# A Mamba decoder block on one core: two of five scan steps get dt*u*B by transposes, the other products are one operation of 1024, and the task planner gets new durations

## What is computed

```python
x = layernorm(x + mamba(mamba(x)))            # two Mamba layers, D_INNER 512, 64 states
x = layernorm(x + attention(x, ctx))          # 256 keys, one head, Wq Wk Wv Wo
x = layernorm(x + experts(x))                 # 8 experts, hidden 1024, the two best weighted

# inside a Mamba layer, for each of 512 channels d and 64 states s:
dt = softplus(...)                            # per channel and time
h[t] = exp(dt[t] * A[d, s]) * h[t-1] + dt[t] * u[t] * B[t, s]
y[t] += h[t] * C[t, s]
```

## Time and profile before

| | |
|---|---|
| median of 3 runs | 3817.08 us (3805.78 to 3820.71) |
| profiled execution | 3814.09 us |
| its span, first to last instruction | 3812.3 us |
| mean granted TensorE clock | 0.894 |
| VectorE, TensorE, ScalarE, GpSimd busy | 89%, 82%, 71%, 68% |

### The profile page before, as it was taken

How to read it: one execution, slowest core, us unless ns; L and a number is a source line. 1 busy time by engine, 2 the same in 40 slices (tenths; PEclk the granted TensorE clock), 3 DMA queues, 4 the chain that set the end, 5 groups by cost and what they waited for, 6 DMA issues and landing times.

```text
span 3812.3 us, 50672 instructions
## 1 busy us (share of the span) xinstructions
PE 3116.1 (82%) x17860; PEld 2582.1 (68%) x17860; DVE 3388.7 (89%) x4041; ACT 2703.3 (71%) x6090; POOL 2585.8 (68%) x1216
## 2 busy tenths in 40 slices
PE   5777777778787888878787887888787888888999
PEld 3566666667676767667676776767676676777877
DVE  4999999998999999999999999999999999998100
ACT  5768687776878788777878778786777778676222
POOL 4778777776868677776777677776777678666000
PEclk7777677889898999989899899989999898999999
DMA  2111111112131222212231222312222121323344
GB/s 105 43 41 40 45 43 40 44 40 81 62 105 45 78 84 86 86 42 95 70 105 52 67 81 76 104 47 83 70 92 73 56 88 63 103 82 107 115 141 128
DMA packets 81490, 286.87 MB, mean 75 GB/s; under 512 B 9786, under 2 KB 10819, under 8 KB 80596
## 3 DMA queue, kind: packets, MB, share of 16 engines
q1 hardware_dynamic: 80210, 281.21, 22.5%
q10 hardware_dynamic: 1026, 2.42, 0.2%
HBM read 280.44 MB, written 3.15 MB: 74 GB/s over the span
## 4 chain that ended last, share of the span: by engine, by line
DVE 31%; POOL 27%; issue 24%; PE 13%; ACT 3%; DMA 2%; POOLq 0%; SPq 0%; DVEq 0%
POOL hC L613 24%; DVE h L835 23%; DVE psX L825 5%; PE psY L1067 4%; PE psG L1023 3%; POOL scratch L564 2%; PE psG L1094 2%; DMA wexp<-in_w_exp 1%; PE psX L1051 1%; ACT dA L803 1%; PE psX L1023 1%; POOL dtu L580 1%; DVE acc L885 1%; PE psX L1094 1%; ACT xs L777 0%
## 5 line engine op out<-in xcount | busy, mean ns | idle before, releaser
L613 POOL TENSOR_TENSOR hC<-h,cb 128x1024 f32<-128x1024 f32 x1024 | 2406.0, 2362 | 907.4 <-DVE h L835 815.3
L835 DVE TENSOR_TENSOR_SCAN h<-dA,psX 128x512 f32<-128x512 f32 x2048 | 2367.1, 1203 | 28.7 <-PE psX L1051 26.9
L803 ACT ACTIVATE dA<-dt,negA 128x255 f32<-128x255 f32 x4096 | 1726.8, 500 | 388.6 <-DVE h L835 385.7
L1067 PE MATMUL psY<-ident,hC 128*128 128x128 f32 x8192 | 1266.2, 305 | 419.9 <-POOL hC L613 368.0
L1067 PEld LDWEIGHTS psY<-ident,hC 128*128 128x128 f32 x8192 | 1061.2, 157 | 657.2 <-POOL hC L613 539.9
L825 DVE TENSOR_TENSOR psX<-dtu,psX 128x512 f32<-128x512 f32 x1384 | 949.3, 686 | 86.1 <-PE psX L1042 61.7
L1051 PE MATMUL psX<-ident,xs 128*128 128x128 f32 x2656 | 417.7, 310 | 84.2 <-DVE h L835 42.6
L1023 PE MATMUL psG<-x2T,wexp 128*128 128x256 f32 x1680 | 447.1, 395 | 24.9 <-DVE gl L961 9.9
L1094 PE MATMUL psG<-wexp,hid 128*128 128x256 f32 x1664 | 433.7, 385 | 20.5 <-DVE acc L885 12.5
L777 ACT ACTIVATE xs<-dtuT,bT 128x512 f32<-128x512 f32 x664 | 441.1, 716 | 0.2
L1051 PEld LDWEIGHTS psX<-ident,xs 128*128 128x128 f32 x2656 | 360.7, 162 | 106.5 <-ACT xs L777 54.2
(11 more groups left out here) (157 smaller groups left out, 1828.8 us busy)
## 6 DMA issues: line engine op xcount, KB each, us to landing
wexp<-in_w_exp SPq DMA_DIRECT2D x256, 512.0 KB, 3.6
cb<-c_dram SPq DMA_DIRECT2D x256, 512.0 KB, 3.7
xin<-in_xT SPq DMA_DIRECT2D x8, 256.0 KB, 4.2
w_in<-in_w_in SPq DMA_DIRECT2D x2, 1024.0 KB, 7.8
ctxT<-in_ctxT SPq DMA_DIRECT2D x8, 256.0 KB, 4.0
xrow<-in_x SPq DMA_DIRECT2D x8, 256.0 KB, 4.1
y<-acc SPq DMA_DIRECT2D x8, 256.0 KB, 3.4
w_x<-in_w_x SPq DMA_DIRECT2D x1, 1088.0 KB
```

Of the source, the lines that this page charges most:

```text
L613: eng.tensor_tensor(hC[i % NHC][:, :, :], h[i % NH][:, :, :], cw.to_broadcast([P, KI, L]), ALU.mult).then_inc(times_c, 1)
L803: made = eng.activation(dA[j % NA][:, c, 1:L], dt[n % 2][:, c, 1:L], ACT.Exp, scale=negA[:, JOBS[n][0], c, s:s + 1])
L835: eng.tensor_tensor_scan(h[i % NH][:, 2 * f:2 * f + 2, :].rearrange("p c t -> p (c t)"), dA[i % NA][:, 2 * f:2 * f + 2, :].rearrange("p c ...
L1067: made = eng.matmul(psY[:, tc, c * P:(c + 1) * P], hC[i % NHC][:, c, tc * P:(tc + 1) * P], ident[:, :], start=s == 0 and c == 0, stop=Fals ...
```

## The change

`is_turned` takes every step i with i mod 5 equal to 1 or 3 (i above 12), counted over all steps and not within a job: 405 turned steps, 619 plain. The product of a plain step is one instruction of 1024 elements, and both halves of the scan wait for it. The planner's constants change, and the modelled delay from a task to its successor is now `HOP`, 120 ns in place of 60. A relu waits until the output products of the pair two before it are done, since it overwrites what they read.

```diff
 def is_turned(i):
-    return i % S % 3 == 2 and i > 12
+    return i % 5 in (1, 3) and i > 12

-MM, TURN, EVICT, HALF_EVICT = 440, 125, 620, 470
-WINDOW, PE_OVER, FIRST = 24, 0, 1500
+MM, TURN, EVICT, HALF_EVICT = 260, 130, 620, 450
+WINDOW, PE_OVER, FIRST, HOP = 24, 0, 1500, 120

-        at = max([self.at[t.eng]] + [self.done[x] + 60 for x in t.needs])
+        at = max([self.at[t.eng]] + [self.done[x] + HOP for x in t.needs])
...
-        return (None, None) if k is None else (max(at, self.bank_at[k] + 60), k)
+        return (None, None) if k is None else (max(at, self.bank_at[k] + HOP), k)

                         on.wait_ge(full[k], at + 1)
+                        on.wait_ge(out_pair, weights_at(n, e, p) - 1)
                         for i in range(2):
                             made = eng.activation(hid[p % 2][:, i, :], ...

-                for f in range(2):
-                    on.wait_ge(times_b, 2 * PLAIN_TO[i] + f)
-                    eng.tensor_tensor(x[:, 2 * f:2 * f + 2, :], dtu[n % 2][:, 2 * f:2 * f + 2, :],
-                                      x[:, KI - 1:KI, :].to_broadcast([P, 2, L]), ALU.mult).then_inc(times_b, 1)
+                eng.tensor_tensor(x[:, :, :], dtu[n % 2][:, :, :], x[:, KI - 1:KI, :].to_broadcast([P, KI, L]),
+                                  ALU.mult).then_inc(times_b, 1)

             def scan(i, f):
...
-                    on.wait_ge(times_b, 2 * PLAIN_TO[i] + f + 1)
+                    on.wait_ge(times_b, PLAIN_TO[i] + 1)
```

## The result

The changed kernel takes 4029.1 us (median of four, 4022.9 to 4034.9) against 3818.3 for the kernel before in the same runs: ratio 1.056, 95% interval 1.053 to 1.059. I had forecast 3690. Its profiled execution has a span of 4021.1 us.

A forecast was written before the change was run, and what follows sets the result against it. VectorE was taken to bound the loop and TensorE the tail. From 3812 us of span, 96, 43 and 83 came off and 95 was added: 3685 us of span, 3690 us of time; range 3590 to 3840.

The forecast's parts named there:

- The tail gets less work: Tail: 24 expert pairs leave it, at 3.46 us of TensorE each, 83 us less; bounds 0 and 110.
- the new durations: Planner: MM 260 for 440 packs TensorE to 17.5 us per five loop steps where VectorE needs 15.7; 95 us more.
- My remark on the clock: TensorE: more work per step keeps the granted clock at its upper level, a few microseconds off, none counted.
- Packing in the loop: Loop: low-priced products make TensorE the bound in fully packed steps; 95 us more, bounds 0 and 166.
- The third rival: Loop: in-order TensorE stops for relus, VectorE idles; 3889 us at 1.4 us a pair, chance 0.14.
- VectorE's own work: Loop: VectorE's busy time falls from 3351 to 3212 us, 139 us less, by more turned steps and merging.
- The merged product: Plain steps on VectorE: one product of 1024 takes 1.23 us, scan starts at 1.24 for 1.31; 43 us gain.
- The turned steps: Loop on VectorE: 73 more steps without a product, each saving 1.32 us; 96 us gain.
- The signs named: Loop: VectorE's wait for psX grows from 87 to some 180 us; tail: relus fall from 140 to 92.
- the packing term: Loop: 95 us of stalls from TensorE tasks packed too full; wrong if VectorE's psX wait stays near 87 us.
- the slower rival: Loop: TensorE's in-order queue stops for relus not yet begun; ends above 3836, 3889 us at 1.4 a pair, chance 0.14.
- my cases: Whole kernel: forecast 3640 to 3750 (0.5), light packing 3620 (0.23), gain given back 3803 (0.13), slower 3889 (0.14).

The follow-up runs named there:

- The first two experiments: Changed kernel with only the tail planned at 440 ns per product: 3833.0 us; changed kernel with four expert weight buffers for three: 3825.5 us.
- the old rule at the new price: Changed kernel with every third step of a job turned, MM 260, HOP 100, tail planned at 440: 3989.6 us, ratio 1.046 to the kernel before.
- 123 at price 360: Changed kernel with every third step of a job turned, MM 360, HOP 120, tail planned at 440: 3850.9 us, ratio 1.011 to the kernel before.
- the middle price: Changed kernel, two of five turned, MM 360 in place of 260, tail planned at 440: 3739.9 us, ratio 0.980 to the kernel before.
- At price 360: Changed kernel with MM 360, four weight buffers, tail planned at 440: every third step of a job turned 3728.7 us, two of five 3717.0 us.
- 340: Changed kernel, two of five turned, MM 340, four weight buffers, tail planned at 440: 3696.4 us, ratio 0.968 to the kernel before.

## Why the prediction was wrong

The forecast of the span was 3685 us and the span is 4021: 336 us off. 183 are the tail's, 153 the loop's.

**The tail.** "The tail gets less work" was right in its count: 92 relus, as forecast. The step that failed is the price behind it, "in the tail a pair costs TensorE 4 x 0.865 = 3.46 us", and the new durations were charged to the steps of the loop alone. I followed the low price into the loop and not into the tail, where the planner has three small banks and took a product to be so short that the next pair's `hid` always came first. I forecast 83 us less; it was 100 us more. The first two experiments show the mechanism: three open pairs on three buffers expose the load, in this list the whole of it, and with the wait TensorE's clock falls to half. Of the 6.7 us that a pair takes more, 3.7 are the load and 3.0 the clock. My remark on the clock, that more work per step raises it, held in part of the loop: before 850 us, where no experts run, it is 0.82 for 0.76, behind that 0.92 as before. In the tail it is 0.75 for 0.99.

**Packing in the loop.** The mechanism was the one I named, and the old rule at the new price shows it without the added turned steps (317 us of waits, 123 at price 360, 87 before). The size was wrong: I took 95 us for a term whose bound I had worked out as 166, and VectorE's idle time grew by 208. The bound counted only that TensorE's sum of work exceeds VectorE's. It averaged over five steps, and the close-up shows what that leaves out: tasks come in clumps, there of 4.3 us where a step has room for 2.5. Steps with four or more expert tasks are 24 in the list before, 74 after, and 91 with the old rule at 260. They are not the whole account: the middle price has 24 again, and 185 us of waits, for 123 with the old rule, so that the turned steps, each of which takes 0.88 of TensorE for 0.12, have a part. How much each has was not measured. The third rival's mechanism, TensorE stopping for relus, is not it: these stops take 19 us of the loop before and after.

**VectorE's own work.** The merged product was right: 1.21 for 1.23, start to scan 1.24 as worked out, and alone it brought 44 us of loop and 41 of the time (48 expected for 692 products). The whole busy time fell by 100 us and not by 139. About half of the difference is, by estimate, that a scan or product behind an idle stretch can't overlap the one before: 216 more waits at 0.09 us are 19 us. Another 8 us are work on the pairs that moved from the tail (35.0 to 27.4 us there). The last 12 stay unexplained.

**The turned steps.** I credited 96 us in full and let nothing of it go to TensorE. At price 360 they bring 27 us of loop and about 12 of the whole time.

**The signs named.** I wrote that the waits would be some 180 us, that near 87 the packing term would be wrong and above 300 the slower rival would hold. They are 291. Slower it is, but not by that rival's mechanism and not at its 3889 us: the loss is the packing, at more than its bound, and a slower tail, which none of my cases had.

## What to carry to other kernels

A planner's duration sets the order of work everywhere it is used. Before a cheaper price is credited with the work it moves, ask of every stage how many buffers the new order keeps in use at once, whether any is left to be loaded, and how much work stands between the moment one comes free and the moment its load is needed. A duration below the measured one is a way to place more work, good while the engine has room: here 340 for 430 measured paid, 260 did not. And a bound from sums of work is no upper bound when the queue is in order; tasks that arrive in clumps cost more.

## What the runs showed of the hardware

The four tasks of a pair ran at two very different rates. Where TensorE waited 1.8 us for weights it mostly kept 2.4 GHz (granted clock 1.00 in the stretch shown, 0.91 to 1.00 in windows of 20 us from 3696 to 3836 of that run) and a pair took 5.6 us. Where it waited 3.7 us the granted clock fell to 0.50 within the wait, so that three of the four tasks ran at 1.2 GHz, and a pair took 10.2: 3.7 us more for the wait and 3.0 for the clock. The Trainium skill, "TensorE: Matmul & The Clock Gate", Part 1, describes these two levels and that waits for DMA make the clock fall; the trace agrees, with 1.7 us against 0.865 for the same task.

On VectorE the scan that depends on a product of 1024 starts 0.03 us after its end (1.24 beside 1.21), while a scan that does not depend on the product before it starts 0.09 before that one's end (1.31 beside 1.40 in the earlier trace rows).
